# Reordering the bridge between the two passes of a fused attention and feed-forward kernel on eight cores

## The chip, the cores and the metric

The kernel runs on the 8 cores of one Trainium2 chip, one batch element on each, without traffic between the cores. The metric is the device time of the slowest core in microseconds (us). The engines of a core are TensorE (PE, with its weight loads PEld), VectorE (DVE), ScalarE (ACT), GpSimd (POOL) and SyncE (SP, which here only issues transfers). They run their own instruction streams and wait for each other by semaphores.

## The reference

Each of 8 batch elements has 4096 rows (tokens) of D = 1024 numbers; 16 heads of 64; FF = 4096.

```python
src = layernorm(x)
Q, K = elu(src @ Wq + bq) + 1, elu(src @ Wk + bk) + 1
V = src @ Wv + bv
KV = einsum('bshd,bshm->bhdm', K, V)
Z = 1 / (einsum('bshd,bhd->bsh', Q, K.sum(axis=1)) + EPS)
o = einsum('bshd,bhdm,bsh->bshm', Q, KV, Z)
x1 = layer_norm(src + o @ Wo + bo, g1, be1)
y = gelu(x1 @ W1 + b1) @ W2 + b2
x = x + layer_norm(x1 + y, g2, be2)
n = layernorm(x)
out = x + n @ weight.T + pooled(n) @ disha
```

## The kernel before

**First pass** (`sync_a`, `pool_a`, `act_a`, `dve_a`, `pe_a`). T = 32 tiles of 128 rows. Per tile t: load x, normalise it (`norm`), transpose it by DMA into `srcT` (a group of four tiles shares one of three buffers), and project K and V on PE (`proj`, 16 matmuls of 512 columns each). K gets elu + 1 (`k_in` on DVE, `k_exp` on ACT, `k_out` on DVE), V is copied (`v_out`), and `kv_sum` adds K'V of the tile to PSUM. GpSimd sums K over the tiles into `kacc` (`k_sum`). Q is projected in blocks, transposed: block n of 64 covers 128 of the 1024 outputs for four tiles (`q_proj`, 8 matmuls of 512 columns), lags one group behind, and is evicted by `q_exp` (ACT) and `q_out` (DVE) into the staging `qst[0]`, `qst[1]`; `q_store` writes four blocks at a time to memory. Tiles 4 to 27 carry two Q blocks each; the last 16 (from Q0 = 48) are left over. GpSimd issues the loads of all weights with a cast: Wk, Wv, Wq at the start, W2 in 32 rows' blocks (`w2_load`), Wo and the first quarter of W1 during the tiles.

**Bridge** (`sync_f`, `pool_f`, `act_f`, `dve_f`, `pe_f`, lines 893 to 1116). The last 16 Q blocks are mixed with work that depends on the finished sums, in an order written out by hand for each engine: K's column sums by matmuls with ones over `kahi` and `kalo` (the two bf16 halves of `kacc`), the block-diagonal `kvz` from KV plus bias terms (DVE, lines 1023 to 1032), M = kvz @ Wo in 16 matmuls (`m_proj`) into four banks, emptied by ACT and DVE in turn (`m_out`), the denominators of supertiles 0 and 1 (`den`), their reciprocals by Ln and Exp on ACT (`z_inv`) and the scaling of Q by them on DVE (`z_mul`), the attention output of supertile 0 (`attn`), its first layer norm (`t_add`, `t_stats`, `t_rstd` on GpSimd, `x1`), the cast of x1 to bf16 (`x1_cast`) and its transposition on PE (`x1_tr`, `x1_out`).

**Second pass** (`sync_b` to `pe_b`). 16 supertiles of 256 rows, block i for feed-forward of supertile i. A block has 32 chunks c: eight matmuls of 256 columns of the first layer (line 1317), GELU on ACT, and a step later four matmuls of 512 columns of the second layer (`y_step`, line 1295). At fixed chunks the attention of supertile i + 1, the final projection of supertile i - 1 and the denominators of supertile i + 2 are put in between; those are inverted by `q_scale` (a reciprocal and a product per quarter, DVE). Block 0 also waits for the four quarters of W1 at chunks 0, 8, 16, 24, and during it SP and GpSimd build the last weight matrix: 16 loads of `WfT` through a ring of two halves and 16 `w_sum` additions (line 1169). `bo_add` and `b2_add` add bias rows on GpSimd.

Within an engine everything runs in the written order, so a wait holds up all that is behind it. The waits of the second-layer step for its weights, and the two that now stand ahead of the transposed x1 of supertile 1:

```python
            if n == 0:
                te.wait_ge(s_w2, 16 * (NFCH - 1))
                te.wait_ge(f_ln, 8)
                te.wait_ge(a_qe, NCH * NG)
...
            if j == 1:
                sc.wait_ge(s_qst[0], 32 * NG)
                sc.wait_ge(s_qst[1], 32 * NG)
```

## Time and profile before

| | us |
|---|---|
| median of 3 runs (lowest, highest) | 1547.5 (1546.93, 1549.16) |
| the profiled execution, whole | 1548.03 |
| its span, first to last instruction, slowest core | 1546.5 |
| spans of the eight cores | 1540.5 to 1546.5 |
| mean granted clock of TensorE | 0.990 to 0.992 |
| PE busy | 1499.4 (97%) |
| DVE, ACT, POOL busy | 965.9, 520.8, 420.9 |

The profile is one execution on the slowest core (core 1). Its page gives busy time by engine, the span in 40 slices of 38.7 us with a digit for tenths of busy time, the granted clock of TensorE in tenths of full speed and the share of the 16 DMA engines. Further views list waits (who waited for whom), the instructions in order of time, busy time in chosen windows, and DMA issues with the time from issue to landing. Matmuls are pipelined: the end of a group is modelled, and the start of the next is the better mark.

### The profile page before, as it was taken

Reading aid. Unit: us, or ns where it says so; the run is one execution under the profiler, and the core shown is the slowest. Engines: PE = TensorE matmul, PEld = TensorE weight load, DVE = VectorE, ACT = ScalarE, POOL = GpSimd, SP = SyncE. Lnnn points to the kernel's source line nnn. Section 1 sums busy time; section 2 is a strip of 40 time slices with the busy share of each in tenths; the row PEclk is TensorE's granted clock in tenths of the full one; section 3 lists DMA queues with packets and bytes.
Section 4 is the critical chain, followed back from the end, with each engine's and each line's share of the span. In section 5 each row is a group of like instructions: output and inputs, shape, how many; then the busy total and the mean of one; then the engine's idle time right before and its main releaser. Section 6 shows DMA issues by size and latency. Waiting matters only on the chain.

```text
span 1546.5 us, 26550 instructions; the slowest of 8 cores (1540.5 to 1546.5 us)
## 1 busy us (share of the span) xinstructions
PE 1499.4 (97%) x9220; PEld 890.2 (58%) x9220; DVE 965.9 (62%) x1076; ACT 520.8 (34%) x929; POOL 420.9 (27%) x406
## 2 busy tenths in 40 slices
PE   5999999997799999999999999999999999999997
PEld 2444444443366666666666666666666666666664
DVE  4666666656638576576758575666767585765334
ACT  2444444435533323232323323232323333232221
POOL 3223233233463222223122222222231222222111
PEclk9999999999899999999999999999999999999999
DMA  9979988899552313223131312121221223121121
GB/s 200 201 180 191 203 192 195 178 208 200 121 138 68 89 49 76 56 82 68 56 89 49 96 48 77 52 85 49 76 76 59 81 54 89 49 76 56 56 69 41
DMA packets 141024, 157.52 MB, mean 102 GB/s; under 512 B 94688, under 2 KB 102880, under 8 KB 140896
## 3 DMA queue, kind: packets, MB, share of 16 engines
q1 hardware_dynamic: 120112, 123.58, 28.3%
q0 software_dynamic: 14112, 25.70, 12.0%
q10 hardware_dynamic: 6672, 6.56, 1.3%
q8 instruction: 78, 1.28, 0.3%
q14 instruction: 50, 0.41, 0.1%
HBM read 117.53 MB, written 41.94 MB: 103 GB/s over the span
## 4 chain that ended last, share of the span: by engine, by line
PE 76%; DMA 13%; DVE 5%; issue 2%; ACT 1%; POOL 1%; SPq 1%; DVEq 0%; ACTq 0%; POOLq 0%
PE psH L1317 29%; PE psY L1295 28%; DMA arena<-x 10%; PE psS L690 7%; PE psS L871 7%; DMA arena<-Wv 2%; DVE arena L480 2%; PE psY L591 2%; PE psS L562 1%; DVE arena L459 1%; DVE arena L460 1%; PE psS L778 1%; PE psY L562 1%; DMA arena<-arena 1%; SPq L274 0%
## 5 line engine op out<-in xcount | busy, mean ns | idle before, releaser
L1317 PE MATMUL psH<-arena 128*128 128x256 bf16 x4096 | 531.6, 273 | 1.4 <-ACT arena L768 1.4
L1295 PE MATMUL psY<-arena 128*128 128x512 bf16 x2000 | 515.6, 379 | 0.7 <-DVE arena L811 0.4
L1223 ACT ACTIVATE arena<-psH,arena 128x256 bf16<-128x256 f32 x512 | 242.8, 474 | 755.9 <-PE psH L1317 753.9
L1317 PEld LDWEIGHTS psH<-arena 128*128 128x128 bf16 x4096 | 401.0, 98 | 144.9 <-issue 1.6
L1295 PEld LDWEIGHTS psY<-arena 128*128 128x128 bf16 x2000 | 195.6, 98 | 128.4 <-issue 2.0
L799 DVE RECIPROCAL arena<-arena 128x512 f32<-128x512 f32 x56 | 187.4, 3346 | 54.3 <-ACT arena L789 54.3
L591 PE MATMUL psY<-arena 128*128 128x512 bf16 x944 | 212.7, 379 | 2.3 <-DMA arena<-arena 1.3
L591 PEld LDWEIGHTS psY<-arena 128*128 128x128 bf16 x944 | 90.9, 98 | 107.2 <-issue 3.0
L739 POOL TENSOR_TENSOR arena<-arena 128x1024 f32<-128x1024 f32 x32 | 69.0, 2155 | 237.6 <-ACT arena L735 237.6
L699 DVE TENSOR_TENSOR arena<-psS,arena 128x512 f32<-128x512 f32 x60 | 41.4, 690 | 147.4 <-PE psS L690 147.2
L328 POOL TENSOR_TENSOR arena<-arena 128x1024 f32<-128x1024 f32 x31 | 71.4, 2302 | 209.4 <-DVE arena L497 208.9
L685 POOL TENSOR_TENSOR arena<-arena 128x1024 f32<-128x1024 f32 x32 | 68.6, 2147 | 215.2 <-ACT arena L680 215.2
L690 PE MATMUL psS<-arena 128*128 128x512 bf16 x480 | 114.4, 382 | 0.0
L871 PE MATMUL psS<-arena 128*128 128x512 bf16 x480 | 113.4, 379 | 0.0
L562 PE MATMUL psS<-arena 128*128 128x512 bf16 x448 | 106.1, 380 | 0.0
L811 DVE TENSOR_TENSOR arena<-psY,arena 128x512 f32<-128x512 f32 x64 | 40.0, 684 | 80.4 <-PE psY L1295 80.4
L823 POOL TENSOR_SCALAR arena<-arena 128x1 f32<-128x1 f32 x32 | 21.2, 663 | 233.1 <-DVE arena L819 190.4
L878 DVE TENSOR_TENSOR arena<-psS,arena 128x512 f32<-128x512 f32 x60 | 40.1, 687 | 69.2 <-PE psS L871 69.2
L690 PEld LDWEIGHTS psS<-arena 128*128 128x128 bf16 x480 | 47.2, 98 | 57.4 <-issue 1.4
L871 PEld LDWEIGHTS psS<-arena 128*128 128x128 bf16 x480 | 47.0, 98 | 56.6
L562 PEld LDWEIGHTS psS<-arena 128*128 128x128 bf16 x448 | 43.9, 98 | 52.4 <-issue 0.6
L719 DVE SCALAR_TENSOR_TENSOR arena<-arena 128x1024 f32<-128x1024 f32 x32 | 66.4, 2076 | 1.7
(131 smaller groups left out, 1323.7 us busy)
## 6 DMA issues: line engine op xcount, KB each, us to landing
arena<-x SPq DMA_DIRECT2D x64, 512.0 KB, 5.4
xb_s<-arena SPq DMA_DIRECT2D x32, 512.0 KB, 6.2
arena<-W POOLq DMA_DIRECT2D x64, 256.0 KB, 7.1
arena<-xb_s SPq DMA_DIRECT2D x32, 512.0 KB, 3.2
out<-arena SPq DMA_DIRECT2D x31, 512.0 KB, 3.0
arena<-qt_s SPq DMA_DIRECT2D x16, 512.0 KB, 3.7
qt_s<-arena ACTq DMA_DIRECT2D x24, 256.0 KB, 9.1
arena<-WfT SPq DMA_DIRECT2D x16, 256.0 KB, 3.0
```

The costliest lines, as they stand in the source:

```text
L328: gp.tensor_tensor(kacc[:, :], kacc[:, :], k_buf(t)[:, :], ALU.add).then_inc(a_ks, 1)
L562: ii = te.matmul(q_bank(n), wq_v[:, w, c * P:(c + 1) * P], srcT[g % 3][:, w, :], start=(w == 0), stop=(w == NCH - 1))
L591: ii = te.matmul(ps[:, nh * 512:(nh + 1) * 512], srcT[(t // 4) % 3][:, w, lo:lo + P], wgt[:, w, nh * 512:(nh + 1) * 512], start=(w == 0), ...
L685: gp.tensor_tensor(home(j, sub)[:, :], home(j, sub)[:, :], bob[:, :], ALU.add).then_inc(b_bo, 1)
L690: ii = te.matmul(bank, qbuf(j)[:, sub, c, :], m_v[:, c, nh * HALF:(nh + 1) * HALF], start=(c == 0), stop=(c == NCH - 1))
L719: v.scalar_tensor_tensor(hm[:, :], hm[:, :], mvt[sub][:, 0:1], g1b[:, :], ALU.subtract, ALU.mult).then_inc(b_gt, 1)
L739: gp.tensor_tensor(home(j, sub)[:, :], home(j, sub)[:, :], b2b[:, :], ALU.add).then_inc(b_b2, 1)
L799: v.reciprocal(ring(j, k), ring(j, k)).then_inc(b_rc, 1)
L871: ii = te.matmul(bank, nT[:, c, :], wf_v[:, c, nh * HALF:(nh + 1) * HALF], start=(c == 0), stop=(c == NCH - 1))
L1223: sc.activation(h_buf(n)[:, :], hbank[n % 2], AF.Gelu, bias=b1c[:, c:c + 1]).then_inc(b_g, 1)
L1295: ii = te.matmul(ybank[k], h_buf(n)[:, (k // 2) * P:(k // 2 + 1) * P], w2_v[c][:, (k % 2) * HALF:(k % 2 + 1) * HALF], start=(c == 0), stop ...
L1317: ii = te.matmul(hbank[n % 2], w1_v[c // NCH][:, w, (c % NCH) * P:(c % NCH + 1) * P], x1T[i % 2][:, w, :], start=(w == 0), stop=(w == NCH ...
```

## The change

Six of the last 16 Q blocks are projected in tiles 28 to 30, two per tile; ten are left (QL = 54). K's sum on GpSimd ends with tile 29; `last_prep` on DVE splits it ahead of tile 31's K, and the K of tiles 30 and 31 enter the matmuls with ones directly. The products for `kvz` come ahead of the denominators' part; M follows one Q block behind. The copies of M are divided 6 to ACT and 10 to DVE. Attention of supertile 0 waits chunk by chunk. Everything of supertile 1 (denominators, scaling, `bo_add`, normalised x) leaves the bridge; its denominators are written into the place of `qst[1]`, inverted on DVE as those of later supertiles, at chunks 2 to 8 of block 0, and its attention moves from chunks 0 and 1 to 12 and 13. Some steps of block 0 move on by one or two chunks. The loads of `g1`, `be1`, `qs1` and of W1 and the last five blocks of W2 are issued at other points. Removed lines of the three long lists are those of the functions printed above.

```diff
+            if j == 1:
+                return VF(W + 40960 + 2048 * (k % 2), HALF)
-        q_last = [sbank[0], ybank[2], sbank[0], ybank[3]]
+        QL = NCH * NG - 10
+        q_last = [sbank[0], ybank[2], ybank[3]]
-            return sbank[n % 2] if n < NCH * (NG - 2) else q_last[n % 4]
+            return sbank[n % 2] if n < QL else q_last[(n - QL) % 3]
...
-                w2_load(t - 6)
+                if t < 28:
+                    w2_load(t - 6)
-                    w2_load(t + 2)
+                    w2_load(t - 2)
-            for t in range(4, T):
+            for t in range(4, T - 2):
...
-                if 7 <= t < T - 4 and t % 4 == 3:
+                if t >= 7 and t % 4 == 3:
-                if 5 <= t < T - 4:
+                if 5 <= t < T - 1:
-                if t < T - 4:
+                if t < T - 1:
...
+        def last_prep(v):
+            v.wait_ge(a_q, NCH * (NG - 2))
+            v.memset(kvz[:, :], 0.0).then_inc(f_mem, 1)
+            v.memset(ksb[:, :, :], 0.0).then_inc(f_mem, 1)
+            v.wait_ge(a_rstd, T)
+            v.scalar_tensor_tensor(nm0c[:, :], m0c[:, :], -1.0, r0c[:, :], ALU.mult,
+                                   ALU.mult).then_inc(f_nm, 1)
+            v.wait_ge(a_ks, T - 2)
+            for k in range(2):
+                v.wait_ge(s_tr[k], 16 * (T // 2 - 3))
+            v.tensor_copy(kahi[:, :], kacc[:, :]).then_inc(f_hi, 1)
+            v.wait_ge(f_hi, 1)
+            v.tensor_tensor(kalo[:, :], kacc[:, :], kahi[:, :], ALU.subtract).then_inc(f_lo, 1)
...
+                if t == T - 1:
+                    last_prep(v)
-                if t < T - 4:
+                if t < T - 1:
-                if t < T - 4:
...
-                sc.wait_ge(s_qst[0], 32 * NG)
-                sc.wait_ge(s_qst[1], 32 * NG)
+                sc.wait_ge(b_qh, 4)
-            sc.wait_ge(b_den, 4 * (j - 2) + k + 1)
+            sc.wait_ge(b_den, 4 * (j - 1) + k + 1)
-                sc.wait_ge(b_qh, 4 * (j - 2) + k - 1)
+                sc.wait_ge(b_qh, 4 * (j - 1) + k - 1)
+            elif j == 1:
+                sc.wait_ge(s_qst[1], 32 * NG)
...
+            sy.wait_ge(f_ks, 1)
+            sy.dma_start(qs1[:, :, :, :], qt_d[1]).then_inc(s_q1, 16)
+            gp.wait_ge(s_bo, 16)
+            bo_add(gp, 0, 0)
+            bo_add(gp, 0, 1)
+            gp.wait_ge(f_kvz, 2)
+            t_rstd(gp, 0, 0)
+            t_rstd(gp, 0, 1)
+            gp.wait_ge(a_qt, NCH * NG)
+            for c in range(27, NFCH):
+                gp.dma_start(w2_v[c][:, :], w2_d[c * P:(c + 1) * P, :]).then_inc(s_w2b, 16)
+            def z_inv(k):
+                sc.wait_ge(f_den, k + 1)
+                if k >= 2:
+                    sc.wait_ge(f_q, k - 1)
+                sc.activation(zring[k % 2], sbank[1], AF.Ln, bias=EPS_Z).then_inc(f_ln, 1)
+                sc.wait_ge(f_ln, k + 1)
...
+            q_exp(sc, QL)
+            m_out(0)
+            m_out(2)
+            z_inv(0)
+            m_out(4)
+            m_out(6)
+            q_exp(sc, QL + 1)
+            z_inv(1)
+            m_out(8)
+            q_exp(sc, QL + 2)
+            z_inv(2)
+            m_out(12)
+            q_exp(sc, QL + 3)
+            z_inv(3)
+            q_exp(sc, QL + 4)
             x1_cast(sc, 0, 0)
+            q_exp(sc, QL + 5)
+            q_exp(sc, QL + 6)
+            x1_cast(sc, 0, 1)
             x1_out(sc, 0, 0, sbf[1])
+            q_exp(sc, QL + 7)
+            x1_out(sc, 0, 1, hbf)
+            q_exp(sc, QL + 8)
+            q_exp(sc, QL + 9)
 
         def dve_f(v):
...
+            v.wait_ge(s_rows, 48)
+            v.wait_ge(f_kr, 1)
+            v.wait_ge(a_kb, T)
+            for r in range(2):
+                x, y = r * DH, (r + 1) * DH
+                bcol = bvc[x:y, :]
+                bb = bass.AP(bcol.tensor, bcol.offset, [list(bcol.ap[0]), [1, NCH], [0, DH]])
+                v.tensor_tensor(ztmp[x:y, :, x:y], ksr[x:y, :, x:y], bb, ALU.mult).then_inc(f_kv, 1)
+            v.wait_ge(f_mem, 2)
+            v.wait_ge(a_kv, T)
+            for r in range(2):
+                x, y = r * DH, (r + 1) * DH
+                v.wait_ge(f_kv, r + 1)
+                v.tensor_tensor(kzp[x:y, :, x:y], kvp[x:y, :, x:y], ztmp[x:y, :, x:y],
...
+                                ALU.add).then_inc(f_kvz, 1)
+                x, y = r * DH, (r + 1) * DH
+                kcol = kscol[x:y, :]
+                v.tensor_copy(ksb[x:y, :, x:y], kb).then_inc(f_ksz, 1)
+            m_out(1)
+            m_out(3)
+            q_out(v, QL)
+            z_mul(0)
+            m_out(5)
+            m_out(7)
+            q_out(v, QL + 1)
+            z_mul(1)
+            m_out(9)
+            m_out(10)
+            m_out(11)
+            q_out(v, QL + 2)
+            z_mul(2)
+            m_out(13)
+            m_out(14)
+            m_out(15)
+            q_out(v, QL + 3)
+            z_mul(3)
+            t_add(v, 0, 0, 0, mbank[0])
+            t_add(v, 0, 0, 1, mbank[1])
+            t_stats(v, 0, 0)
+            q_out(v, QL + 4)
+            x1(v, 0, 0)
+            t_add(v, 0, 1, 0, ybank[0])
+            t_add(v, 0, 1, 1, ybank[1])
+            t_stats(v, 0, 1)
+            q_out(v, QL + 5)
+            x1(v, 0, 1)
+            for n in range(QL + 6, NCH * NG):
+                q_out(v, n)
...
+            def m_group(k):
+                for j in range(4 * k, 4 * k + 4):
+                    m_proj(j)
+            def den_0(k):
+                if k >= 1:
+                    te.wait_ge(f_ln, k)
+                den(te, 0, k, sbank[1], f_den)
+            def attn_00(nh):
+                for c in range(NCH):
+                    if c == 0:
+                        m_done(te, 12 + nh)
+                    m_done(te, 2 * c + nh)
+                    if c % 2 == 0:
+                        te.wait_ge(f_q, c // 2 + 1)
+                    ii = te.matmul(mbank[nh], qs[:, 0, c, :], m_v[:, c, nh * HALF:(nh + 1) * HALF],
+                                   start=(c == 0), stop=(c == NCH - 1))
+                ii.then_inc(b_at, 1)
+            sums = (kahi, kalo, kbf[0], kbf[1])
+            te.wait_ge(a_kb, T - 1)
+            for part in sums:
+                if part is kbf[1]:
+                    te.wait_ge(a_kb, T)
+                for nh in range(2):
+                    ii = te.matmul(psK[:, nh * 512:(nh + 1) * 512], onesb[:, :],
+                                   part[:, nh * 512:(nh + 1) * 512], start=(part is kahi),
+                                   stop=(part is kbf[1]))
+            ii.then_inc(f_kr, 1)
+            kv_sum(te, T - 1)
+            te.wait_ge(a_qe, QL)
+                for part in sums:
+                    ii = te.matmul(ps_ks[:, c:c + 1], part[:, c * P:(c + 1) * P], onesb[:, 0:1],
+                                   start=(c == 0 and part is kahi),
+                                   stop=(c == NCH - 1 and part is kbf[1]))
+            q_proj(te, QL)
+            m_group(0)
+            q_proj(te, QL + 1)
+            te.wait_ge(s_q, 16)
+            te.wait_ge(f_kc, 1)
+            te.wait_ge(f_ksz, 2)
+            den_0(0)
+            m_group(1)
+            q_proj(te, QL + 2)
+            den_0(1)
+            m_group(2)
+            q_proj(te, QL + 3)
+            den_0(2)
+            m_group(3)
+            den_0(3)
+            attn_00(0)
+            attn_00(1)
+            q_proj(te, QL + 4)
+            m_done(te, 14)
+            m_done(te, 15)
+            attn(te, 0, 1, 0, ybank[0])
+            attn(te, 0, 1, 1, ybank[1])
+            q_proj(te, QL + 5)
+            q_proj(te, QL + 6)
+            q_proj(te, QL + 7)
+            x1_tr(te, 0, 1, hbf)
+            q_proj(te, QL + 8)
+            q_proj(te, QL + 9)
...
-                sy.wait_ge(f_q, 8)
+                sy.wait_ge(f_q, 4)
-                sy.wait_ge(b_qh, 4 * (i + 1))
+                sy.wait_ge(b_qh, 4 * (i + 2))
...
+                w_sum(0)
+                w_sum(1)
+                bo_add(gp, 1, 0)
+                w_sum(2)
+                w_sum(3)
+                bo_add(gp, 1, 1)
+                for h in range(4, 10):
+                    w_sum(h)
+                w_sum(10)
+                w_sum(11)
+                gp.wait_ge(s_b2, 16)
+                for j in range(2):
+                    b2_add(gp, j, 0)
+                    b2_add(gp, j, 1)
...
-                if c == (16 if post else 14) and pre:
+                if c in (3, 4, 6, 8) and not post:
+                    den_out(sc, 1, c // 2 - 1, sbank[0 if c in (3, 6) else 1])
+                if c in (5, 7) and not post:
+                    src_norm(sc, 1, (c - 5) // 2)
+                if c == (16 if post else 18) and pre:
...
+            else:
+                for k in range(4):
+                    q_scale(v, 1, k)
...
-                te.wait_ge(s_w2, 16 * (NFCH - 1))
-                te.wait_ge(f_ln, 8)
+                te.wait_ge(s_w2, 16 * 27)
-            if n == NFCH - 1:
-                te.wait_ge(s_w2, 16 * NFCH)
+            if n == 27:
+                te.wait_ge(s_w2b, 16 * (NFCH - 27))
-                if c == 0 and pre:
-                    if i >= 1:
-                        te.wait_ge(b_qh, 4 * i)
-                        te.wait_ge(b_de, 4 * i)
-                    else:
-                        te.wait_ge(f_q, 8)
-                        te.wait_ge(a_qe, NCH * NG)
+                if c in (2, 3, 5, 7) and not post:
+                    if c == 2:
+                        te.wait_ge(s_q1, 16)
+                    elif c >= 5:
+                        te.wait_ge(b_de, c // 2 - 1)
+                    den(te, 1, c // 2 if c > 2 else 0, sbank[0 if c in (2, 5) else 1], b_den)
+                if c == (0 if post else 12) and pre:
+                    te.wait_ge(b_qh, 4 * (i + 1))
+                    te.wait_ge(b_de, 4 * (i + 1))
-                if c == 1 and pre:
+                if c == (1 if post else 13) and pre:
...
```

## Rows read from the trace of the kernel before

**Rows 1.** The page: busy tenths and granted TensorE clock in 40 slices of the span.

```profile
PE   5999999997799999999999999999999999999997
...
PEclk9999999999899999999999999999999999999999
```

**Rows 2.** Waits of PE, 330 to 470 us: us in total, times, longest.

```profile
PE psS L759 <- ACT arena L735: 8.0, 2, 4.1
...
PE psH L1061 <- DVE arena L997: 4.2, 1, 4.2
```

**Rows 3.** PE in order of time: start, us, what, [idle before, releaser].

```profile
303.81 3.62 PE L591 MATMUL psY<-arena 128*128 128x512 bf16 x16
...
314.62 7.07 PE L591 MATMUL psY<-arena 128*128 128x512 bf16 x32
...
338.60 7.07 PE L591 MATMUL psY<-arena 128*128 128x512 bf16 x32 [1.25 <-DMA arena<-arena]
...
381.25 5.17 PE L690 MATMUL psY<-arena 128*128 128x512 bf16 x16 [3.38 <-DVE arena L793]
...
420.10 1.03 PE L1295 MATMUL psY<-arena 128*128 128x512 bf16 x4
...
457.85 1.04 PE L1317 MATMUL psH<-arena 128*128 128x256 bf16 x8
```

**Rows 4.** Window (busy us, counts; clock, DMA) and timeline of DVE.

```profile
346.44:350.96 4.52, 4.52 (x29) 2.28 (x28) 4.06 (x6) 2.19 (x4) 3.26 (x3) 1.00 0.73 235
...
368.40 0.69 DVE L793 TENSOR_TENSOR arena<-arena 128x512 bf16<-128x512 bf16 x1
...
369.00 0.69 DVE L997 CAST arena<-psH 128x512 bf16<-128x512 f32 x1
```

**Rows 5.** Timelines of DVE and POOL, each with the other beside it.

```profile
361.12 5.45 DVE L448 SCALAR_TENSOR_TENSOR arena<-arena 128x512 bf16<-128x512 bf16 x1 [0.86 <-ACT arena L369]
...
361.73 4.28 POOL L685 TENSOR_TENSOR arena<-arena 128x1024 f32<-128x1024 f32 x2
...
450.80 0.69 DVE L699 TENSOR_TENSOR arena<-psS,arena 128x512 f32<-128x512 f32 x1 [2.77 <-PE psS L690]
...
449.60 2.49 POOL L1169 TENSOR_TENSOR arena<-arena 128x512 bf16<-128x512 f32 x2
```

**Rows 6.** Timelines of DVE and ACT: x1 of supertile 0, first GELU.

```profile
386.59 0.69 DVE L699 TENSOR_TENSOR arena<-psY,arena 128x512 f32<-128x512 f32 x1 [1.03 <-PE psY L690]
...
391.74 2.88 DVE L723 SCALAR_TENSOR_TENSOR arena<-arena 128x1024 f32<-128x1024 f32 x1 [0.18 <-DVE arena L719]
...
411.23 1.04 ACT L735 ACTIVATE arena<-arena 128x1024 bf16<-128x1024 f32 x1
...
416.85 1.28 ACT L1223 ACT_TABLE_LOAD   x1 [2.31 <-PE psH L1317]
```

**Rows 7.** DMA landings (stores at 359 to 360, 411, all; disha; b2), window.

```profile
DMA to landing us min/median/max: 9.9/11.8/13.7
...
qt_s<-arena SPq DMA_DIRECT2D x2, 256.0 KB, 3.4
...
DMA to landing us min/median/max: 2.5/8.2/15.5
...
arena<-disha SPq DMA_DIRECT2D x1, 512.0 KB, 9.2
...
arena<-b2r POOLq DMA_DIRECT2D x1, 256.0 KB, 21.8
...
420.00:430.00 10.00, 10.00 (x67) 6.29 (x65) 5.94 (x7) 2.37 (x5) 3.20 (x4) 1.00 1.06 209
```

**Rows 8.** Timelines of SP and DVE: loads of WfT, scaling of supertile 2.

```profile
415.97 46.19 SPq L1133 DMA_DIRECT2D arena<-WfT  x16
...
460.76 3.35 DVE L799 RECIPROCAL arena<-arena 128x512 f32<-128x512 f32 x1 [1.36 <-ACT arena L789]
...
478.02 0.69 DVE L793 TENSOR_TENSOR arena<-arena 128x512 bf16<-128x512 bf16 x1
```

More of the change, by code:

```diff
@@ L161, in build_nc @@
         s_wq, s_wo = sema("wq_in"), sema("wo_in")
-        s_w2, s_w1 = sema("w2_in"), [sema("w1_in%d" % j) for j in range(4)]
+        s_w2, s_w2b, s_w1 = sema("w2_in"), sema("w2_in_last"), [sema("w1_in%d" % j) for j in range(4)]
         s_x = [sema("x_in%d" % k) for k in range(8)]
@@ L891, in build_nc, with m_done @@
         zring = [slot[4][:, 0:HALF], slot[4][:, HALF:D]]
+        M_ACT = [0, 2, 4, 6, 8, 12]
+        M_DVE = [j for j in range(2 * NCH) if j not in M_ACT]
+        def m_done(eng, j):
+            if j in M_ACT:
+                eng.wait_ge(f_me, M_ACT.index(j) + 1)
+            else:
+                eng.wait_ge(f_md, M_DVE.index(j) + 1)
         def sync_f(sy):
@@ L1009, in dve_f, with z_mul @@
-            v.wait_ge(a_ks, T)
-            for k in range(2):
-                v.wait_ge(s_tr[k], 16 * (T // 2 - 3))
-            v.tensor_copy(kahi[:, :], kacc[:, :]).then_inc(f_hi, 1)
-            v.wait_ge(f_hi, 1)
-            v.tensor_tensor(kalo[:, :], kacc[:, :], kahi[:, :], ALU.subtract).then_inc(f_lo, 1)
-            for n in range(3):
-                q_out(v, Q0 + n)
+            def z_mul(k):
+                v.wait_ge(f_z, k + 1)
+                q_hat(v, 0, k, zring[k % 2], f_q)
@@ new lines, in dve_f @@
+            kvp, kzp, ztmp, ksr = chunks(psH), chunks(kvz), chunks(zf), chunks(psK)
+            v.wait_ge(s_rows, 48)
[7 more added lines that the diff above has]
+            v.wait_ge(f_mem, 2)
@@ L1047, in dve_f @@
-            q_out(v, Q0 + 12)
-            z_mul(1, 0)
-            for k in range(1, 4):
-                q_out(v, Q0 + 12 + k)
-                z_mul(1, k)
+                v.tensor_copy(ksb[x:y, :, x:y], kb).then_inc(f_ksz, 1)
[11 more added lines that the diff above has]
+            q_out(v, QL + 2)
@@ L1071, in pe_f @@
             te.wait_ge(a_z, T)
-            for nh in range(2):
-                for part in (kahi, kalo):
-                    te.matmul(psK[:, nh * 512:(nh + 1) * 512], onesb[:, :],
-                              part[:, nh * 512:(nh + 1) * 512], start=(part is kahi),
-                              stop=(part is kalo))
+            te.wait_ge(a_kb, T - 1)
[6 more added lines that the diff above has]
+                                   stop=(part is kbf[1]))
@@ L1369, in pe_b @@
                     final(te, i - 1, 1, 1, sbank[1])
-                if c == 18 and not post:
+                if c == 19 and not post:
                     te.wait_ge(b_t, 4 * (i + 1) + 3)
                     x1_tr(te, 1, 0, sbf[0])
-                if c == 20 and far:
+                if c == (20 if post else 21) and far:
                     te.wait_ge(s_q, 16 * (i + 2))
@@ L1379, in pe_b @@
                     den(te, i + 2, 0, sbank[0], b_den)
-                if c == 21 and far:
+                if c == (21 if post else 22) and far:
                     if post:
```

187 lines of the change are left out of this document (31 added, 156 removed).

## The prediction

> **What bounds the kernel now.** Three views were read in this order. The slices [rows 1]: TensorE (PE) is full everywhere but at the start, the end and in slices ten and eleven, roughly 345 to 425 us. That is the bridge between the passes. The waits of PE [rows 2] name what it waits for there, first of all 8.0 us for the cast of x1 and 4.2 for DVE's copies of M. The timeline of PE [rows 3] adds a second loss: behind a 3.38 us gap (for the last scaled Q) the sixteen matmuls of 381.25 take 5.17 us where sixteen take 3.62 at 303.81, part of them at the lower of the clock's two levels, 1.2 GHz; the granted clock falls to 8 tenths in the eleventh slice [rows 1]. From 338.60 (K of tile 31) to 420.10 (first second-layer matmul of feed-forward block 0, "y0" below) lie 81.5 us. The PE work in it at 1.73 us per 8 wide matmuls (a quarter of the 32 at 338.60, without the pipelined end): K and V 6.9, 16 Q blocks 27.6, two KV sums 0.9, K's sums 1.3, 8 denominators 1.7, 16 M matmuls 3.5, five attention halves 8.6, transposes 0.9, two first-layer chunks 1.7: 53.1. So 28.4 us are lost, idle or to the slow clock.
>
> **Common ruler.** Call s the start of K of tile 31, 338.60 now. The change's order and today's have done the same PE work when first-layer chunk 20 of block 0 starts, at 457.85 now [rows 3], save K's longer sums. I work out this point for the new kernel.
>
> **1. Six Q blocks into tiles 28 to 30.** A tile with two Q blocks takes 10.81 us (303.81 to 314.62 in [rows 3]), without idle. From K of tile 28 at 314.62 three such tiles give s = 314.62 + 3 x 10.81 = 347.05, so 8.45 later for 6 x 1.73 = 10.4 us of work: 1.9 us of today's idle in the tail is filled. ACT and DVE do the same per tile as before and are not the bound in these tiles. One ACT store of Q (two issues) moves to tile 31, where ACT idles. The w2 loads taken from these tiles relieve the DMA queues.
>
> **2. K's sums ahead.** DVE now does two memsets, the cast and the subtraction ahead of tile 31's k_in, not behind its k_out. The block took 346.44 to 350.96 [rows 4], 4.5 us. It can start when the last Q of tile 30 is evicted, s + 2.0, so k_in starts at s + 6.5, 2.9 behind the end of K's matmuls. The last K is then ready at s + 10.35 (add 1.2, exponential 1.1, min and max 1.2, and the signals). PE, done with V and KV of tile 30 at s + 7.35, does six of the eight sum matmuls and waits 1.7 us in all: a new wait. Four more wide and sixteen more one-column matmuls cost 0.9 + 0.4. DVE's four half-products end at s + 13.6. PE reaches M at s + 13.85, behind one Q block: no wait. What is under way then is GpSimd's bo_add twice, s + 11.1 to s + 15.4. In [rows 5] a DVE operation with two SBUF inputs that began just ahead of such a pair took 5.45 us, while one that reads PSUM took 0.69 in the middle of a GpSimd pair. The half-products read PSUM or PSUM and SBUF, so I take 0. If they were locked out all the same it is +4.5.
>
> The Trainium skill (SBUF — State Buffer, § SBUF: two separate sides) has the same for a DVE operation with two SBUF inputs and extends it to two-port modes, by which the small casts for K's sums would wait until s + 15.4; the denominator that needs them comes at s + 16.4, so the sum is the same by page or row.
>
> **3. M.** From s + 14.8 DVE has ten copies, four q_out and four scalings, 18 x 0.60 = 10.8 us (a scaling and a copy in [rows 4]: 0.69 each, 0.60 from start to start); waits for the pairs Ln, Exp on ACT add 3.0. The last scaling ends at s + 28.6. PE loses 1.6 us on copies, 0.5 and 2.1 at the first attention half. Today the same stretch loses 4.2 + 3.4 and two falls of the clock. Behind s + 28.6: 2 matmuls, half, Q, two halves, Q, Q, transpose, Q: PE ends at s + 41.7. x1 of the second subtile: its adds start at s + 37.6 behind x1 of the first; from its second add to the end of x1 5.7 us ([rows 6]: 386.59 to 391.74, and some 1.3 for the product when GpSimd does not hold it up, less 0.7 of waiting for ACT), cast 1.05: s + 45.0. So PE idles 3.3 us ahead of the second transpose. That is the size of the gap that was followed by slow matmuls in [rows 3], +1.5 for two Q blocks (a loss of nothing to 2.7). ACT then has copy, Q, copy, Q, Q, and GELU's table load of 1.28 [rows 6]: first GELU done, y0 at s + 53.5 by ACT alone, **s + 55** with the slow clock = 402.0. In y0's place PE idles another 1.5 to 2.8 us, since the attention that covered the table load today is gone from there.
>
> **4. Block 0: the new wait that decides.** The denominators of supertile 1 are now written to the upper half of the Q staging (qst[1]), so den_out(1, 0) on ACT waits for the landing of all Q stores. Queued behind it on ACT are GELU 4 and with it y4 on PE. The last store is issued when q_out(63) is done, s + 53.1, second issue 0.75 later. Landing after issue, from [rows 7]: 3.4 us with quiet queues, 9.9 and 13.7 behind a burst of W1 loads. In the new order W1's third quarter is issued at about s + 42, its fourth when the last Q ends, about s + 50, and w2's last five behind it, so the burst stands (at a DMA share of 1.06 it moves 209 GB/s [rows 7]; W1's quarter 2 MB, w2 1.25, stores, Q, disha 1.5 in all take 23 us). The disha load issued 0.4 us behind such a burst landed in 9.2 [rows 7]. I take **11 us**: S = s + 65 = 412. Bounds 3.4 and 15.5, the latter the longest of these stores in the stretch.
>
> The Trainium skill (DMA: Bandwidth & Descriptors, § Issuing engines are not separate DMA queues) says transfers from all engines interleave on the same 16, which speaks against moving W1 and w2 next to this store; [rows 7] agree.
>
> From S: den_out 0.7, then four reciprocals and scalings on DVE, 460.76 to 478.70 = 17.9 [rows 8], so attention(1, 0, 0) at chunk 12 starts at S + 18.7. Unhindered PE would be there at y0 + 21 = s + 76; now it is s + 83.7: 7.7 us of idle, most of it at chunks 4 and 12. From there 19 us of PE work lead to the transpose at chunk 19, S + 37.7. The x1 ahead of it needs t_rstd(1, 0) on GpSimd, which is moved behind ten w_sums and two bo_adds. W's loads are chained to S as today: first issued 415.97, the tenth sum ends 452.1 (449.60 + 2.49 in [rows 5]), 36.1 later. With dsh and bo_adds (hidden in GpSimd's idle) t_rstd ends at S + 37.5, x1 at S + 38.7, cast S + 39.7, transpose done **S + 40.3**: 2 us more. Den(2, 0) moves two chunks nearer the block's end on ACT; its scalings end where attention(2, 0, 0) starts, +0.8 (0 to 3).
>
> **Sum.** Chunk 20 starts at 412 + 40.3 = 452.3, with 0.8 more 453.1, against 457.85: 4.8 us earlier, I take 5. What was won ahead of block 0 is larger: y0 at 402.0 instead of 420.1, minus one attention half and four denominators still to do (2.6), is 15.5; some 10.5 go back in block 0. The profiled execution took 1548.0 us (span 1546.5), 0.5 above the median of the runs. Forecast 1543.0 on its scale, **1542.5** against the median.
>
> **Rivals.**
> (a) *The store lands in a quiet queue*, 3.4 us: S = s + 57.3. Then w_sum lags, since the burst outlasts it; cast and transpose at about S + 44 = 448.3, +0.8: 449.1, a gain of 8.7, and 10 to 11 if w_sum keeps its pace. 1537 to 1539. For it: the pair issued at 411 landed so [rows 7]. Against it: W1 then came before or after them, not with them.
> (b) *Slower*: the store is starved. At 16 us the gain is 0; beyond it every us is lost in full, as ACT, GELU and PE stand in line. The longest landing in the bridge was 21.8 us, of b2 behind W1 [rows 7]: S = s + 75.7, chunk 20 at 463.1 + 0.8, 6 us later: 1553.5. The decision point for slower by over 0.2% is a landing of 19 us. For it: same queues, larger burst. Against: the stores of Q never took over 15.5.
> (c) *The front does not close*: the half-products lock with GpSimd (+4.5), or the two idles of the M stretch both drop the clock (+2 to 3). Then y0 and S move with it: 1546 to 1547. Against: the 0.69 of [rows 5]. This is also the case that the change does not do what it says.
>
> **How the numbers follow.** Forecast case (landing 8 to 14 us) 0.46, times 1539.5 to 1545.5; (a) 0.24; (b) 0.13, of which 0.10 is slower in measure; (c) 0.17, nearly all no change, some slower in company with a late store. What a measurement of this kernel can tell from no change is about 0.2%, 3.1 us: below 1544.4 or above 1550.6. Faster: 0.37 of the forecast case, 0.23 of (a), 0.01 of (c): 0.61. Slower: 0.10 + 0.03 = 0.13. Same: 0.26. Range, leaving out half of (b) and the last part of (a): 1536.5 to 1550.5.
>
> **What would show it.** Right: K of tile 31 starts near 347 without idle; PE waits under 2 us ahead of K's sums; about 3 us ahead of the second x1 transpose; y0 near 402; ACT's den_out of supertile 1 waits for a DMA qt_s<-arena up to about 412; PE waits at chunk 12 for a DVE scaling; chunk 20 near 453. Wrong: no such wait on the store (then (a)); chunk 12 released by something other than the scalings; PE gaps over 4 us between s + 11 and s + 30; w2's last five or W1's fourth quarter late, which I hold to be 25 us early; or time lost in blocks 1 to 15, which I take as unchanged.

## The result, and the profile after

The changed kernel takes **1555.15 us** (median of five executions, 1554.3 to 1555.9) where the kernel before takes 1549.04 beside it: ratio 1.0041, 95% interval 1.0026 to 1.0056. It is slower by 6.1 us, outside the range of the prediction. The profiled execution took 1555.3 us, and its trace is read on its longest core (span 1553.4).

Timeline of PE in the changed kernel, as in [rows 3] (start, us, what, idle before and releaser):

```profile
347.86 7.07 PE L611 MATMUL psY<-arena 128*128 128x512 bf16 x32
...
357.86 0.59 PE L1124 MATMUL psY<-arena 128*128 128x512 bf16 x2 [1.11 <-DVE arena L518]
...
376.38 2.36 PE L1111 MATMUL psH<-arena 128*128 128x512 bf16 x10 [1.75 <-DVE arena L814]
...
393.18 0.61 PE L779 MATMUL psH<-arena 128*128 128x128 bf16 x8 [3.63 <-ACT arena L755]
...
403.40 1.38 PE L1357 MATMUL psY<-arena 128*128 128x512 bf16 x4 [2.73 <-ACT arena L1279]
...
417.49 1.81 PE L1357 MATMUL psY<-arena 128*128 128x512 bf16 x4 [4.86 <-ACT arena L1279]
...
434.61 1.89 PE L710 MATMUL psS<-arena 128*128 128x512 bf16 x8 [1.83 <-DVE arena L814]
...
461.96 1.01 PE L779 MATMUL psS<-arena 128*128 128x128 bf16 x8 [8.13 <-ACT arena L755]
462.77 1.91 PE L1379 MATMUL psH<-arena 128*128 128x256 bf16 x8
```

The first five are the bridge. It closes as the change says: the 4.2 us for DVE's copies of M and one of the two 4 us waits for a cast of x1 [rows 2] are gone, and y0 starts at 403.40 where it started at 420.10 [rows 3]. The last four lines are block 0, which was free of waits before. Chunk 20 starts at 462.77 and not at 457.85: all that was won is given back, and 4.9 us more. Here are the instructions that decide it, first SP's, ACT's, then GpSimd's and DVE's:

```profile
401.21 1.23 SPq L381 DMA_DIRECT2D qt_s<-arena  x2
...
416.37 0.34 SPq L1175 DMA_DIRECT2D arena<-disha  x1
416.81 52.73 SPq L1181 DMA_DIRECT2D arena<-WfT  x16
...
473.58 0.42 SPq L694 DMA_DIRECT2D arena<-x  x1
```

```profile
416.38 0.60 ACT L810 ACTIVATE arena<-psS 128x512 f32<-128x512 f32 x1 [6.82 <-DMA qt_s<-arena]
...
460.76 1.06 ACT L755 ACTIVATE arena<-arena 128x1024 bf16<-128x1024 f32 x1 [8.90 <-DVE arena L743]
...
481.33 1.24 ACT L700 ACTIVATE arena<-arena 128x1024 f32<-128x1024 f32 x1
```

```profile
428.48 1.26 POOL L1217 TENSOR_TENSOR arena<-arena 128x512 bf16<-128x512 f32 x1 [14.88 <-DMA arena<-WfT]
...
456.13 1.26 POOL L1217 TENSOR_TENSOR arena<-arena 128x512 bf16<-128x512 f32 x1 [1.76 <-DMA arena<-WfT]
457.36 0.22 POOL L731 TENSOR_SCALAR arena<-arena 128x1 f32<-128x1 f32 x1
457.73 0.57 POOL L734 TENSOR_TENSOR arena<-arena 128x1 f32<-128x1 f32 x1
```

```profile
458.41 2.20 DVE L743 SCALAR_TENSOR_TENSOR arena<-arena 128x1024 f32<-128x1024 f32 x1 [13.18 <-POOL arena L734]
```

The last Q store lands 14.5 us after issue, and den_out (L810) waits for it. The tenth w_sum starts at 456.13; t_rstd behind it releases DVE, DVE the cast, the cast PE. The last line of ACT is src_norm of supertile 2 (L700): it doesn't wait (x landed 4.7 us after its issue, at 478.3), since everything before it is late too. The windows 400 to 470 us (busy us and counts of PE, PEld, DVE, ACT, POOL; granted clock, DMA share, GB/s), first of the changed kernel, then of the kernel e11 below, show the loss once more: 52.45 against 66.59 us of PE work, and a granted clock of 0.90 against 0.98.

```profile
400.00:470.00 70.00, 52.45 (x318) 32.43 (x316) 31.08 (x24) 18.96 (x35) 33.30 (x34) 0.90 0.70 146
```

```profile
400.00:470.00 70.00, 66.59 (x448) 43.39 (x446) 46.10 (x31) 28.06 (x50) 39.56 (x37) 0.98 0.73 156
```

In many executions of e7 to e16, of the kernel before too, two or more cores stood at a granted clock of 0.98 or less and took 12 us longer or more, and the ratios leave out only the worst of these, so beside a ratio stands the median of the n executions in which all eight cores were above 0.987 ("undisturbed": before 1547.8 to 1549.2 on each chip, n 8 to 17).

### The profile page after: what moved, and what is told of

Same layout as the page of the kernel before. It is cut to its first block, busy times and chain, and to the rows that moved or that the text cites. A ratio compares the mean times of both kernels' runs of the same rounds, so it can differ in the third digit from the quotient of the medians.

```text
span 1552.0 us, 26610 instructions; the slowest of 8 cores (1546.1 to 1553.4 us)
## 1 busy us (share of the span) xinstructions
PE 1497.2 (96%) x9240; PEld 889.7 (57%) x9240; DVE 977.3 (63%) x1082; ACT 516.4 (33%) x923; POOL 418.4 (27%) x404
## 3 DMA queue, kind: packets, MB, share of 16 engines
q0 software_dynamic: 14112, 25.70, 12.3%
q8 instruction: 78, 1.28, 0.3%
## 4 chain that ended last, share of the span: by engine, by line
PE 88%; DMA 5%; DVE 3%; issue 2%; POOL 2%; ACT 1%; SPq 0%; DVEq 0%; ACTq 0%; POOLq 0%
PE psH L1379 27%; PE psY L1357 26%; PE psY L611 12%; PE psS L892 7%; PE psS L710 6%; PE psS L582 6%; DMA arena<-Wv 2%; DMA arena<-WfT 2%; DMA qt_s<-arena 1%; DVE arena L820 1%; PE psH L590 1%; PE psS L797 1%; POOL arena L1217 0%; PE psY L582 0%; POOL arena L356 0%
## 5 line engine op out<-in xcount | busy, mean ns | idle before, releaser
L1379 PEld LDWEIGHTS psH<-arena 128*128 128x128 bf16 x4096 | 402.0, 98 | 143.3 <-issue 0.3
L820 DVE RECIPROCAL arena<-arena 128x512 f32<-128x512 f32 x60 | 200.8, 3346 | 72.1 <-ACT arena L810 72.1
L759 POOL TENSOR_TENSOR arena<-arena 128x1024 f32<-128x1024 f32 x32 | 68.8, 2154 | 230.4 <-ACT arena L755 222.3
L705 POOL TENSOR_TENSOR arena<-arena 128x1024 f32<-128x1024 f32 x32 | 68.1, 2128 | 229.8 <-ACT arena L700 229.8
L333 POOL TENSOR_TENSOR arena<-arena 128x1024 f32<-128x1024 f32 x29 | 67.7, 2333 | 201.8 <-DVE arena L518 201.3
L739 DVE SCALAR_TENSOR_TENSOR arena<-arena 128x1024 f32<-128x1024 f32 x32 | 68.4, 2138 | 1.7
```

Of the source, the lines that this page charges most:

```text
L333: gp.tensor_tensor(kacc[:, :], kacc[:, :], k_buf(t)[:, :], ALU.add).then_inc(a_ks, 1)
L705: gp.tensor_tensor(home(j, sub)[:, :], home(j, sub)[:, :], bob[:, :], ALU.add).then_inc(b_bo, 1)
L739: v.scalar_tensor_tensor(hm[:, :], hm[:, :], mvt[sub][:, 0:1], g1b[:, :], ALU.subtract, ALU.mult).then_inc(b_gt, 1)
L759: gp.tensor_tensor(home(j, sub)[:, :], home(j, sub)[:, :], b2b[:, :], ALU.add).then_inc(b_b2, 1)
L820: v.reciprocal(ring(j, k), ring(j, k)).then_inc(b_rc, 1)
L1379: ii = te.matmul(hbank[n % 2], w1_v[c // NCH][:, w, (c % NCH) * P:(c % NCH + 1) * P], x1T[i % 2][:, w, :], start=(w == 0), stop=(w == NCH ...
```

## The experiments

The quoted expectations use the theories as they stood when each was written; "A" and "B" mean something else in each of e1 to e4, "C" is the chain below, and "D" says that block 0 is full or held by traffic as a whole. The picture that came out is a **serial chain**: last Q store, disha, sixteen WfT loads through the two halves of slot 4 with a w_sum each on GpSimd, x of supertile 2 into the same slot 4, its src_norm on ACT in chunk 28 with GELU 29 queued behind it. On its way it releases den_out (the store) and t_rstd (the tenth w_sum).

**One wait at a time.** e1 moves t_rstd on GpSimd:

```diff
-                for h in range(4, 10):
-                    w_sum(h)
                 t_rstd(gp, 1, 0)
-                w_sum(10)
-                w_sum(11)
+                for h in range(4, 8):
+                    w_sum(h)
                 t_rstd(gp, 1, 1)
+                for h in range(8, 12):
+                    w_sum(h)
```

> Only the order on GpSimd in block 0 is changed: the two t_rstd of supertile 1 come behind the fourth and the eighth w_sum instead of behind the tenth and the twelfth. Theory A (the 8.1 us wait of PE for the cast of x1 is due to t_rstd queued behind w_sum, whose loads start only when all Q stores have landed): the reciprocal root ends near 445 us instead of 458.3, the wait ahead of the transpose at chunk 19 vanishes with the slow matmuls behind it (8.1 + 1.3), chunk 20 starts near 454 instead of 462.8; about 9 us under the changed kernel, so 3 us under the kernel before. Theory B (block 0 is late because supertile 1's denominators and scalings run in it at all; the next link takes the wait over): under 3 us gained, the kernel stays slower than before.

Ratio 1.0033 (1.0020 to 1.0047), undisturbed 1553.7 (n 4). The 8.1 us wait vanished; PE's transpose came at 453.72. In its place, on ACT and PE of e1:

```profile
477.54 1.24 ACT L700 ACTIVATE arena<-arena 128x1024 f32<-128x1024 f32 x1 [6.50 <-DMA arena<-x]
```

```profile
453.72 0.61 PE L779 MATMUL psS<-arena 128*128 128x128 bf16 x8
...
479.28 1.86 PE L1357 MATMUL psY<-arena 128*128 128x512 bf16 x4 [5.39 <-ACT arena L1279]
```

Of 8.1 us, 1.5 arrived, where theory A had 9. Theory B had the size (under 3, the next link takes over) but didn't name the link, the load of x.

e2 lets GpSimd issue W1's fourth quarter only once the stores have landed:

```diff
             gp.wait_ge(a_q, NCH * NG)
+            gp.wait_ge(s_qst[0], 32 * NG)
+            gp.wait_ge(s_qst[1], 32 * NG)
             for w in range(NCH):
```

> Only one thing is changed: GpSimd waits for the landing of all Q stores before it issues the fourth quarter of W1 (and w2's last five behind it). Theory A (the last Q store lands late because it shares the queues with that burst): the store lands 3 to 5 us after issue instead of 13 to 14.5, ACT's wait of 6.8 us for it and PE's 4.9 us vanish, the loads of WfT start near 406 instead of 416, t_rstd follows them, chunk 20 starts near 452; 9 to 11 us under the changed kernel. Theory B (the store is slow for a reason of its own, its 1 KB pieces or the end of the pass): landing stays above 8 us and less than 4 us is gained.

Ratio 1.0025 (1.0014 to 1.0035), undisturbed 1552.3 (n 8). The landing fell from 14.5 to 8.5 us (theory A had 3 to 5) and PE's 4.9 us at chunk 3 went, but attention(1, 0) at 427.80, 6.8 earlier than in the changed kernel, was followed by 11.3 us of waiting for the cast: the burst, only moved, now lay on the WfT loads (the third and fourth w_sum at 432 and 434, GpSimd idle 5.76 us ahead of them). Less than 4 us was gained, as theory B had it.

e3 gives the denominators two free 2 KB buffers, so that den_out waits for no store (the wait for it now stands ahead of the later x1_out):

```diff
-                return VF(W + 40960 + 2048 * (k % 2), HALF)
+                return VF((W + 55296, W + 34816)[k % 2], HALF)
...
             elif j == 1:
-                sc.wait_ge(s_qst[1], 32 * NG)
```

> Only the place of supertile 1's denominators is changed: they go to two free buffers instead of the Q staging, so ACT does not wait for the Q stores at chunk 3; the loads of WfT still start when the stores have landed. Theory A (two limits hang on the store, and the later one, t_rstd behind w_sum, decides): the 4.9 us wait at chunk 4 vanishes, attention at chunk 12 starts near 427 instead of 434.6, but PE then waits about 15 us instead of 8.1 for the cast of x1, chunk 20 stays near 462.5, and the time is within 1.5 us of the changed kernel. Theory B (the wait of ACT for the store is what costs): 5 to 7 us gained.

Ratio 1.0051 (1.0034 to 1.0068), undisturbed 1556.6 (n 4): nothing gained, as its theory A said. PE's wait for the cast grew from 8.1 to 10.7, and a 3.5 us wait for a bo_add stood before it. **ACT's wait for the store's landing, on which I had put the range, is worth nothing by itself**; the landing still starts the loads of WfT.

e4 is e3 with both bo_adds ahead of the sums and t_rstd behind the second and the fifth:

```diff
+                bo_add(gp, 1, 0)
+                bo_add(gp, 1, 1)
                 w_sum(0)
                 w_sum(1)
-                bo_add(gp, 1, 0)
...
+                t_rstd(gp, 1, 0)
+                for h in range(2, 5):
+                    w_sum(h)
+                t_rstd(gp, 1, 1)
```

> Both at once: denominators in free buffers, and on GpSimd the two bo_adds ahead of all w_sums, the two t_rstd behind the second and the fifth w_sum. The front of the change is untouched, first second-layer matmul near 403. Theory A: no wait for the store, attention at chunk 12 near 427.5 (held by the four scalings of 17.9 us behind the first denominator at 409.6), chunk 20 near 447 to 449; 14 to 16 us under the changed kernel and 8 to 11 us under the kernel before, ratio to before 0.993 to 0.995. Theory B (block 0 with supertile 1 in it is too long by itself): 5 to 8 us under the changed kernel, about even with before.

Ratio 1.0018 (1.0007 to 1.0028), undisturbed 1551.6 (n 8): 3.6 us under the changed kernel, where theory A had 14 to 16. Both waits are gone and PE is at the transpose at 445.53, 16.4 us ahead of the changed kernel; 12.3 us of it are lost in one place. ACT, PE and SP of e4:

```profile
476.23 1.24 ACT L700 ACTIVATE arena<-arena 128x1024 f32<-128x1024 f32 x1 [13.37 <-DMA arena<-x]
```

```profile
445.53 0.61 PE L779 MATMUL psS<-arena 128*128 128x128 bf16 x8
...
477.97 1.86 PE L1354 MATMUL psY<-arena 128*128 128x512 bf16 x4 [12.28 <-ACT arena L1276]
```

```profile
417.00 49.03 SPq L1180 DMA_DIRECT2D arena<-WfT  x16
...
470.13 0.42 SPq L694 DMA_DIRECT2D arena<-x  x1
```

x of supertile 2 is issued at 470.1 however early the rest is. This is the last link.

**Starting the loads early.** SP's wait for the second half of the stores moved behind the loads, in e7 on top of e4, in e8 alone:

```diff
                 sy.wait_ge(s_qst[0], 32 * NG)
-                sy.wait_ge(s_qst[1], 32 * NG)
                 sy.dma_start(dsh2[:, :], dsh_d).then_inc(s_dsh, 16)
...
                 sy.wait_ge(b_ws, 16)
+                sy.wait_ge(s_qst[1], 32 * NG)
                 sy.dma_start(g2b[:, :], g2_d).then_inc(s_g2, 16)
```

> The kernel of e4_ring_and_rstd, and SyncE no longer waits for the store out of qst[1] before it issues disha and the 16 loads of WfT (they overwrite qst[0] and slot 4 only; the wait stands behind them). Theory C, formed from e4 (one chain decides block 0: last Q store, disha, 16 WfT loads through two halves of slot 4, g2, x of supertile 2 into slot 4, its normalisation on ACT at chunk 28 with GELU 29 behind it; 59 us from the store in e4): the chain starts near 403 instead of 416.6, x of supertile 2 lands near 465 or before, e4's 12.3 us wait at the second layer and the slow clock behind it vanish; 11 to 14 us under e4, so 7 to 11 us under the kernel before (ratio 0.993 to 0.9955). Theory D (the wait passes on to the next link once more, block 0 is full): less than 4 us under e4.

> The changed kernel with this one wait of SyncE moved and nothing else. Theory C: the 4.9 us wait at chunk 4 for the store stays, but w_sum and with it t_rstd come 10 us earlier, so PE's 8.1 us wait for the cast of x1 and the slow clock behind it vanish, and the loads of x for supertile 2 are in time; 8 to 10 us under the changed kernel, 2 to 4 us under the kernel before. Theory D: less than 4 us under the changed kernel, still slower than before.

e7: ratio 1.0036 (1.0005 to 1.0066), undisturbed 1551.9 (n 8); e8: 1.0055 (1.0008 to 1.0102), undisturbed 1554.3 (n 5). The loads began 16 and 12 us earlier, at 400.65 and 404.54, but took 65.5 and 60.4 us instead of 49.0 (e4) and 52.7 (the changed kernel): in e8 the second pair of sums came 10 us behind the first (426.41 and 436.83), and in e7 GpSimd stood 10.8 us at t_rstd, two sums done, until 437. x was issued at 470.2 and 469.1. Theory C had 11 to 14 us for e7 and 8 to 10 for e8 and missed both; the times are those of theory D, whose reason e11 and e12 below don't bear out. Two buffers tie the loads to GpSimd's order, so an early start is wasted.

**The front alone** (supertile 1 put back into the bridge, with my own placing of its denominators in the Y banks), e10 with the loads early as well:

```diff
+            te.wait_ge(b_t, 4)
+            den(te, 1, 0, ybank[0], f_den)
             x1_tr(te, 0, 0, sbf[1])
             q_proj(te, QL + 7)
+            den(te, 1, 1, ybank[1], f_den)
```

> One part of the change alone: the new front (six Q blocks in tiles 28 to 30, K's sums ahead, M behind the last V, attention of supertile 0 chunk by chunk, W2's last five late) with supertile 1 back in the bridge and block 0 as in the kernel before. PE's bridge should end some 13 us earlier (first second-layer matmul near 406 to 408 instead of 420.1). Theory C: nothing of it arrives, because the store of the last Q still lands at 415 to 418 and ACT waits 10 to 15 us at chunk 28 for x of supertile 2; 1547 to 1551, within 2 us of before. If that chain does not bind (theory D): 1535 to 1538.

> e9_front_only with SyncE's wait for the qst[1] store moved behind the WfT loads. Theory C: the wait at chunk 28 shrinks to nothing or little, 9 to 13 us under e9 and under the kernel before (ratio 0.992 to 0.995). Theory D: the same time as e9.

Ratios 1.0057 (1.0037 to 1.0076) and 1.0069 (1.0045 to 1.0094), undisturbed 1557.0 (n 1) and 1558.9 (n 2): slower than either theory had them. Neither says much about the front: PE stood 9.1 and 8.2 us at the new denominator, until DVE had read the bank. Both show the last link all the same: 5.9 and 11.1 us of PE behind ACT's wait for x of supertile 2.

**Taking the chain apart.** e11 is e4 with other landing places: WfT's halves go to the last four chunks of the fused weight's own region and one free buffer, five loads can be under way, and x of supertile 2 follows the eighth load. The b2 sums of supertile 0 go ahead of the ninth w_sum.

```diff
+        W_AT = (0, 1, 2, 3, 0, 1, 2, 3, 1, 2, 3, 4, 3, 4, 4, 4)
+        w_half = [VF(REG[5] + 2048 * k, HALF) for k in (4, 5, 6, 7)] + [VF(W + 55296, HALF)]
...
-                    if h >= 2:
-                        sy.wait_ge(b_ws, h - 1)
-                    sy.dma_start(zring[h % 2], wf_d[c * P:(c + 1) * P, lo:lo + HALF]
-                                 ).then_inc(s_wf[h % 2], 16)
+                    if at in W_AT[:h]:
+                        sy.wait_ge(b_ws, h - W_AT[:h][::-1].index(at))
...
+                    sy.dma_start(w_half[at], wf_d[c * P:(c + 1) * P, lo:lo + HALF]
+                                 ).then_inc(s_wf[at], 16)
+                    if h == 7:
+                        sy.wait_ge(f_q, 4)
+                        x_in(sy, 2, 0)
```

> From e4_ring_and_rstd: the halves of WfT land in the last four chunks of the fused weight's own region (and one spare 2 KB buffer) instead of in the two halves of slot 4, so that five loads can be under way, none of them needs the Q stores, and x of supertile 2 is loaded into slot 4 behind the eighth of them instead of behind the sixteenth sum; the b2 sums of supertile 0 move ahead of the ninth sum. Theory C (block 0 is held by one serial chain: last Q store, 16 loads through two halves of slot 4, x of supertile 2, its normalisation ahead of GELU 29): the 13.4 us in which ScalarE waited for x and the 12.3 us of TensorE behind it are gone, x is issued before 450 and the time is 1551.9 - 12 = 1540 (1537 to 1543), below the kernel before (1549). Rival D (the block is held by DMA traffic and SBUF contention as a whole, and the waits only show where that is paid): matmul-side waits turn up elsewhere, 1549 to 1553. If C holds only in part because of a fourth link (the sums in GpSimd's queue ahead of the sums with b2, for which the next block's first y layers wait): a wait of TensorE at chunk 0 of block 1, 1542 to 1546.

> The kernel of e11 once more, for an interval: its first timing stood beside runs of the kernel before of which most were disturbed. Theory C: 1539 (1537 to 1541), 0.993 of the kernel before beside it; ScalarE and TensorE wait nowhere over 1 us between the first y layer and block 1. Rival D: the low time of e11 was the chip's, 0.998 or more.

e11: ratio 0.9862 (0.9737 to 0.9987), undisturbed 1538.8 (n 3). The repeat, e16: **0.9943 (0.9931 to 0.9956)**, undisturbed 1539.2 (n 8). It beats both kernels, the kernel before by 8.6 us. SP, ACT and PE of e11:

```profile
417.37 23.59 SPq L1185 DMA_DIRECT2D arena<-WfT  x8
441.05 0.38 SPq L694 DMA_DIRECT2D arena<-x  x1
445.82 21.73 SPq L1185 DMA_DIRECT2D arena<-WfT  x8
```

```profile
463.26 1.23 ACT L700 ACTIVATE arena<-arena 128x1024 f32<-128x1024 f32 x1
```

```profile
403.66 1.02 PE L1367 MATMUL psY<-arena 128*128 128x512 bf16 x4 [2.77 <-ACT arena L1289]
...
426.98 1.89 PE L710 MATMUL psS<-arena 128*128 128x512 bf16 x8 [0.64 <-DVE arena L813]
...
446.04 0.61 PE L779 MATMUL psS<-arena 128*128 128x128 bf16 x8
446.49 1.04 PE L1389 MATMUL psH<-arena 128*128 128x256 bf16 x8
```

The store lands no sooner and the sixteenth load is issued no sooner (467.6); only x comes 29 us earlier than in e4, and the 12.3 us are gone in full (1551.6 to 1539).

e12 tests the link by one instruction on top of e4:

```diff
-                if c == 28 and far:
+                if c == 28 and far and post:
                     src_norm(sc, i + 2, 0)
+                if c == 1 and i == 1:
+                    src_norm(sc, 2, 0)
```

> From e4_ring_and_rstd, one instruction moved: ScalarE's normalisation of x of supertile 2 goes from chunk 28 of block 0 to chunk 1 of block 1. Theory C: GELU 29 no longer stands behind the DMA, block 0 ends 10 to 12 us earlier; x itself lands at 475 as before, so its bo sum and the attention sum of block 1 come late, and the b2 sums of supertile 0, behind the sixteenth sum at 469.7, hold the first y layer of block 1 for 1 to 3 us: 1541 to 1545. Rival D: nothing is gained, 1550 to 1553.

Undisturbed 1541.5 (n 6, 1540.2 to 1542.4), as theory C said; by the ratio alone, 0.9990 (0.9938 to 1.0042), it couldn't be told from the kernel before. SP and ACT of e12, on core 4:

```profile
466.63 0.42 SPq L694 DMA_DIRECT2D arena<-x  x1
```

```profile
471.04 1.23 ACT L700 ACTIVATE arena<-arena 128x1024 f32<-128x1024 f32 x1
```

x was still issued at 466.6 to 470.5 (cores 3, 4 and 6), but GELU 29 no longer stood behind it: 10 us. So DMA traffic as such (rival D) does not hold the block; an in-order queue behind a late transfer does.

e15 is the same edit in the changed kernel, e13 the loads of e11 in the changed kernel, e14 the same loads in the kernel before.

> The changed kernel with e12's one moved instruction (ScalarE's normalisation of x of supertile 2 at chunk 1 of block 1 instead of chunk 28 of block 0). Theory C: in the changed kernel the waits for the store (4.9 us) and for the cast (8.1 us) come first and x has landed when ScalarE comes to it, so the third link is not on the path yet: 1555 (1553 to 1557), nothing gained. If the instruction's place were worth something by itself, the 10 us of e12 would show here too: 1545.

> The changed kernel with the WfT loads of e11 (their landing places, x of supertile 2 behind the eighth load) and nothing else: the denominators' store wait and GpSimd's order are those of the changed kernel. Theory C: the tenth sum comes 10 us or more earlier (by 447 instead of 457.4), so the cast of supertile 1 isn't late and the 8.1 us of TensorE ahead of chunk 20 and the slow clock behind it go; the 4.9 us for the store at chunk 3 stay: 1555.2 - 8 - 1 = 1546 (1543 to 1549). If only the burst counts (the loads are as slow because W1[3] and the last of W2 are in flight), the sums stay at 450 or later and the time is 1550 to 1555. Rival D: 1553 to 1556.

> The kernel before with the WfT loads and x of supertile 2 as in e11 (landing places, x behind the eighth load), nothing else. Theory C: x of supertile 2 landed 1.9 us ahead of ScalarE's need in the kernel before, so the chain did not yet cost there; freeing it brings nothing: within 1.5 us of the kernel before, and the 10 us between it and e11 are what the change's front and the moved denominators are worth once the chain is gone. Rival E (the loads' new places alone make the gain, the change of the front is worth nothing): 8 to 10 us under the kernel before.

e15: ratio 1.0089 (1.0043 to 1.0136), undisturbed 1554.4 (n 4): nothing gained, as the first two links hide the third. e13: 1.0110 (1.0037 to 1.0183), undisturbed 1549.5 (n 2, so a weak figure), 5.6 under the changed kernel where 9 were expected: the cast's 8.1 us are gone and x is issued at 436, but the store's 4.4 to 5.7 us stay, 1.4 to 2.5 for a scaling at attention(1, 0) with them, and the clock of 400 to 470 us stays at 0.90 to 0.95 (cores 0 to 5). e14: **0.9996 (0.9980 to 1.0012)**, undisturbed 1547.9 (n 6): the loads' new places alone are worth nothing. Hence the 8.6 us of e16 come from the change together with the freed block 0; how much of them is the front's and how much the order of GpSimd's sums and the denominators' place wasn't separated.

## Why the prediction was wrong

**Steps 1 to 3 held.** s was 347.86 (forecast 347.05); PE waited 1.1 at K's sums (1.7), 0.3 at the first M matmul (0), 3.6 ahead of the second x1 transpose (3.3), the following Q block at the slow clock; the half-products did not lock with GpSimd, so rival (c) fell. y0 came at 403.4 (402.0).

**Step 4 named the right waits, missed their sizes, and ended too soon.** Chunk 20 was forecast for 452.3 and came at 462.77, 10.5 late:

- s 0.8 late. The disha load, "S", went at 416.37 and not at 412: 3.5 of the 4.4 us are the store's landing of 14.5 where I took 11. It lay within my bounds, and was longer because the burst I had described lay right on it (DMA share 1.07 from 402 to 412 us; 8.5 us in e2, where W1's last quarter and w2's last five were held back). The rule of the Trainium skill that I had cited (DMA: Bandwidth & Descriptors, § Issuing engines are not separate DMA queues), that transfers of all engines interleave, agrees with these landings, and it spoke against the change.
- From S to the transpose's end I had 40.3 us and it took 46.4. This is the most mis-sized term. I took the pace of the WfT loads and sums from the kernel before: t_rstd ended S + 41.9 instead of 37.5, so 4.4. Some 2.5 of it were there by the fourth sum: the third and fourth loads landed in 7.6 and 8.9 us, where they took 6.6 and 6.1 before. The rest came by the tenth; there the second bo_add (442.03, 2.12 us), which I had called hidden, stood ahead of a sum whose load had landed at 441.5. How much of the rest is its doing wasn't separated. The x1 product took 2.20 beside GpSimd's sums where I had 1.2: the same lock that I had read in [rows 5] for another place, 1.1. The rest is 0.2 in the cast and 0.35 for the transpose, whose eight matmuls took 1.01 instead of 0.61 behind 8.1 us of idle.
- Behind chunk 20 I had 0.8 and it was 2.4 (7.3 us between the two profiled executions, less 4.9 at chunk 20): a wait of 1.58 at attention(2, 0, 0) and the slow clock. Together 12.1 of the 12.3 us between 1543.0 and 1555.3.

**The failed step is the sum of step 4, from the last Q store's issue to chunk 20:** 11 + 40.3 us forecast, 14.5 + 46.4 measured. The waits are the forecast ones, two terms were too small: the landing by 3.5 us, and by 6.1 the path of sixteen loads, w_sum and t_rstd to the transpose. They turn a forecast gain of 4.8 us at chunk 20 into a loss of 4.9.

**A second fault is the choice of chunk 20 as the finish.** It took no part in the 12.3 us, as x of supertile 2 came in time in the changed kernel, but it keeps the gain from arriving as soon as GpSimd's order is put right. "Time lost in blocks 1 to 15, which I take as unchanged" was right, yet chunks 20 to 31 of block 0 lay between. In the kernel before, SP and ACT read:

```profile
468.41 0.42 SPq L674 DMA_DIRECT2D arena<-x  x1
```

```profile
474.63 1.23 ACT L680 ACTIVATE arena<-arena 128x1024 f32<-128x1024 f32 x1
```

x landed in 4.3 us, at 472.7: 1.9 us of slack. The load hangs on the sixteenth w_sum, that on S, and by my own forecast S moved from 415.5 to 412, 3.5 earlier, while chunk 28 was to move 4.8 earlier: 0.6 of slack left (1.9 + 3.5 - 4.8), and none for rival (a), whose w_sums were to lag. So in the forecast case it would just have held. With landings of 14.5 the forecast could not be reached even if t_rstd had been early: e1 and e4 show it, 1553.7 and 1551.6.

**The rivals.** (b) had the sign and the queue (ACT, GELU, PE in line behind the store) but the wrong lever: slower than 0.2% came with a landing of 14.5, not 19, and e3, without that wait, was no faster. No single wait was the lever: the GpSimd order alone gave 1.5 us (e1), the store's wait alone nothing (e3), both 3.6 (e4), and with the load of x freed as well about 16 (e16). The missing rival was the whole chain as one mechanism: the same transfers pass three of PE's suppliers, each next one hidden by the one before. The size of what was won ahead of block 0 was well judged: 15.5 us forecast, 14.1 measured (420.10 less 403.40 and less the same 2.6); 8.6 reach the end in e16.

## What to carry to other kernels

When a bridge is shortened, follow every load that is chained to its end up to its last user, and write the slack of each beside the gain: the gain can't exceed the smallest slack by more than that load itself comes earlier. A buffer ring of two, shared between a stream and the next stage's input, ties that input to the last element of the stream; a landing place in the stream's own, not yet written destination (here with one free 2 KB buffer beside it) unties it. Where the ring isn't on the path it is worth nothing (e14). Where several waits hang on one chain, removing one can show nothing; remove all in one version, and each alone, before a part is called worthless.

## What the runs showed of the hardware

- The last two 256 KB stores of Q, issued from a hardware queue while GpSimd's software queue was emptying 256 KB weight loads (DMA share 1.07), landed in 11.6 and 14.5 us (the last of them in 14.6 to 15.8 in e1, e3 and e4), in 8.2 and 8.5 with thirteen such loads held back (e2), and in 3.4 in quiet [rows 7].
- GpSimd itself was held while it issued such loads: of W1's fourth quarter six went at once and the last two 7.24 us later (6.6 to 10.3 in e1, e3, e4, e7 and e8) with no semaphore to wait for, and what stood behind in its queue waited too. In e2, where the same eight were issued only at 409.89, they went in 4.24 us without a stop. What held them in the others, the runs don't show:

```profile
409.89 1.06 POOL L967 DMA_DIRECT2D arena<-W  x2 [7.24 <-issue]
```

- The DVE product with two SBUF inputs took 1.28 us with GpSimd idle (L739 at 382.60) and 2.20 to 2.24 beside GpSimd's additions (L739 at 442.99, L743 at 458.41 and 465.80).
- PE's idle cost twice: behind 8.1 us of idle the next first-layer chunk took 1.91 us instead of 1.04, and over 400 to 470 us the granted clock was 0.90 with the waits (changed kernel) and 0.98 without (e11).
